# Result rows in four tables by the rank of a token's experts, two of them added early, and the experts' first layer issued one step further ahead

## The reference

```python
x = layernorm(x + attention(x))   # 16 heads of 64, causal, one null key and value, x @ Wo at the end
x = layernorm(x + moe(x))

def moe(xf):                      # xf: 4096 tokens of 128
    scores = softmax(xf @ wg.T)   # 32 experts in 8 groups of 4; the best 4 groups stay,
    w, idx = top 4 of what stays  # and w is divided by its sum
    # every expert takes its first 640 tokens (capacity), in order of the tokens
    h = silu(xe[e] @ w1[e]) * (xe[e] @ w3[e])       # xe: [32, 640, 128]
    y[token] += (h @ w2[e]) * weight of the token
    return y + (silu(xf @ sw1) * (xf @ sw3)) @ sw2  # the shared expert
```

## Time and profile before

| stretch of the trace, us | length | what runs |
| --- | --- | --- |
| 0 to 655 | 655 | attention, router, first scatters |
| 655 to 702 | 47 | last batch's end, first expert |
| 702 to 926 | 224 | 29 experts, 5 scatters each |
| 926 to 960.4 | 34.4 | the tail |

### The profile page before, as it was taken

How to read it: one execution, slowest core, us unless ns; L and a number is a source line. 1 busy time by engine, 2 the same in 40 slices (tenths; PEclk the granted TensorE clock), 3 DMA queues, 4 the chain that set the end, 5 groups by cost and what they waited for, 6 DMA issues and landing times.

```text
span 960.4 us, 26130 instructions
## 1 busy us (share of the span) xinstructions
PE 817.0 (85%) x9489; PEld 594.5 (62%) x9489; DVE 673.9 (70%) x2532; ACT 650.1 (68%) x1262; POOL 681.7 (71%) x580
## 2 busy tenths in 40 slices
PE   4889999999999999999999999873377778786765
PEld 2367777777777777777777777762145555554532
DVE  6667788987987987987897897766255445545417
ACT  3678888888888798898798787864155444444405
POOL 7556565699699689689779869654656576676646
PEclk9799999999999999999999999997789898989979
DMA  5697797743453355345434433133358676566448
GB/s 159 152 297 220 241 249 202 188 121 97 97 147 98 71 140 131 73 108 133 104 90 125 116 80 98 35 91 93 74 117 175 150 168 139 144 152 140 103 157 302
DMA packets 164432, 133.88 MB, mean 139 GB/s; under 512 B 69907, under 2 KB 131654, under 8 KB 163408
## 3 DMA queue, kind: packets, MB, share of 16 engines
q1 hardware_dynamic: 155408, 116.60, 47.4%
q0 software_dynamic: 8896, 15.61, 5.7%
HBM read 31.19 MB, written 39.49 MB: 74 GB/s over the span
## 4 chain that ended last, share of the span: by engine, by line
PE 63%; issue 9%; DVE 7%; DMA 6%; ACT 6%; SPq 5%; another core or an unknown queue 3%; POOL 1%; ACTq 0%; DVEq 0%; POOLq 0%
PE PS L1328 8%; PE PS L1385 6%; PE PS L1359 4%; PE PS L1409 4%; PE PS L1392 4%; PE PS L1390 4%; PE PS L1342 3%; PE PS L1224 3%; PE PS L1411 3%; PE PS L1410 3%; PE PS L1438 3%; PE PS L1439 3%; PE PS L1183 3%; SPq L2503 2%
## 5 line engine op out<-in xcount | busy, mean ns | idle before, releaser
L2328 POOL TENSOR_TENSOR PL<-PF,PH 128x1280 f16<-128x1280 f32 x121 | 317.7, 2626 | 105.6 <-ACT PH L1674 66.6
L1943 DVE CUSTOM_DVE_ANT_0 JUNK<-PS,M 128x256 f16<-128x256 f32 (+3 forms) x512 | 225.3, 485 | 43.6 <-PE PS L1359 40.8
L1668 ACT ACTIVATE PF<-PS 128x512 f32<-128x512 f32 (+1 forms) x384 | 193.2, 520 | 77.3 <-PE PS L1392 74.3
L2371 POOL DMA_INDIRECT y_rows<-BIG,PLACE x150 | 153.0, 1020 | 85.7 <-ACT BIG L1568 48.0
L1674 ACT ACTIVATE PH<-PF 128x1280 f16<-128x1280 f32 x128 | 162.2, 1267 | 0.6
L2361 POOL DMA_INDIRECT xe_rows<-PAY,DEST x128 | 130.2, 1017 | 43.8 <-issue 27.7
L1385 PE MATMUL PS<-Q,K 128*128 128x512 f16 (+3 forms) x512 | 147.9, 299 | 6.9 <-DMA Q<-MROW 3.7
L1409 PE MATMUL PS<-VH,PH 128*128 128x65 f16 x1280 | 140.2, 195 | 11.4 <-DVE Y L1985 7.4
L1411 PE MATMUL PS<-VH,PL 128*128 128x65 f16 x1280 | 140.1, 193 | 0.1
L1410 PE MATMUL PS<-VL,PH 128*128 128x64 f16 x1280 | 140.1, 194 | 0.0
L1409 PEld LDWEIGHTS PS<-VH,PH 128*128 128x128 f16 x1280 | 119.1, 97 | 31.2 <-issue 20.1
(11 more groups left out here) (287 smaller groups left out, 2146.6 us busy)
## 6 DMA issues: line engine op xcount, KB each, us to landing
K<-KH SPq DMA_DIRECT2D x128, 128.0 KB, 2.3
Q<-QH SPq DMA_DIRECT2D x128, 128.0 KB, 2.4
xe_rows<-PAY SPq DMA_DIRECT2D x20, 520.0 KB, 4.1
Q<-xe_rows SPq DMA_DIRECT2D x30, 325.0 KB
K<-KL SPq DMA_DIRECT2D x64, 128.0 KB, 2.3
Q<-QL SPq DMA_DIRECT2D x64, 128.0 KB, 2.4
y_rows<-PAY SPq DMA_DIRECT2D x16, 512.0 KB, 4.9
K<-in_L_ffn_w_dram SPq DMA_DIRECT2D x78, 64.0 KB
```

The costliest lines, as they stand in the source:

```text
L1668: e.activation(PF[:, n % PBUF, c0:c0 + width], PS[:, k, 0:width], ACT.Exp).then_inc(s["c_exp"], 1)
L1943: e.tensor_tensor_reduce(JUNK[:, n_ttr % 2, 0:width], PS[:, base + ab, c0:c0 + width], M0[:, 512 - width:512], 1.0, -3e38, ALU.add, ALU.ma ...
L2328: e.tensor_tensor(PL[:, n % PBUF, :], PF[:, n % PBUF, :], PH[:, n % PBUF, :], ALU.subtract).then_inc(s["c_lp"], 1)
L2371: e.indirect_dma_start(out=y4[:, :], out_offset=bass.IndirectOffsetOnAxis(ap=PLACE[:, x_ % 8, k:k + 1], axis=0), in_=rows_of(x_)[:, k, :], ...
```

## The change

1. **Order of the experts and the row numbers.** `expert(x)` is now 29 - x. The result row is (number of the token's chosen experts whose index is higher) times 4096, plus the token. So `y_rows` is four tables of 4096 rows: table 0 holds each token's result of its highest expert, table 3 that of its lowest. Since the loop goes from high to low, and the experts above 29 take row numbers too without writing them, table 0 is complete after x = 26, table 1 after x = 27. DVE computes the numbers with three new instructions for a batch or half batch ("ahead", "ahead sum", "payi"); POOL's iotas of the payload are gone (four for each batch), one of the setup (TOK) is new.
2. **The tail.** Tables 0 and 1 are loaded by 16 DMAs of 256 KB when they are complete, and DVE adds them to X1 (`share add`, 128x512, both inputs in SBUF). After the last scatter 8 DMAs of 512 KB load tables 2 and 3, half of the bytes of before. PE adds X1 and these two in PSUM; POOL's and DVE's adds are gone, and DVE and ACT read the sum from PSUM.
3. **The loop.** `hidden(x+2)` stands behind `product(x)`, where `hidden(x+1)` stood; `hidden(1)` stands ahead of `product(0)`. Rows split and ring split are of x+3, and the rows of x+4 are loaded ahead of the transpose of x+3. Load ring is still of x+4, so ring split of x+3 now stands one iteration behind its load, where it stood two.

The diff, cut to its core (left out: names, marks, buffers and semaphores, the removed iotas, and ACT's last line, which reads the sum from PSUM):

```diff
@@ -64,7 +64,7 @@
 
 def expert(x_):
 
-    return NE - NA + x_ if x_ < NA else x_ - NA
+    return NE - 1 - x_
@@ -514,6 +514,7 @@
         part("pick", 1)
         yield
         dv("pick sum")
+        dv("ahead sum")
         yield
@@ -522,6 +523,7 @@
                 scatter()
         dv("dest")
         dv("payw")
+        dv("payi")
         yield
@@ -843,22 +846,25 @@
     hidden(0)
     step("set split", 1)
     rows_in(2)
+    hidden(1)
     product(0)
-    hidden(1)
     step("set split", 2)
+    rows_in(3)
     x1_in(1)
-    splits = SPLITS[4:]
+    hidden(2)
+    step("set split", 3)
+    splits = SPLITS[5:]
     forms = list(range(len(WEIGHTS)))
     for x_ in range(1, NE):
-        rows_in(x_ + 2)
-        if NA <= x_ + 2 < NE:
-            step("ring split", x_ + 2)
+        for y_ in range(NA, NA + 2) if x_ == 1 else (x_ + 4,) if x_ + 4 < NE else ():
+            step("load rows", y_)
+        rows_in(x_ + 3)
         if NA <= x_ + 3 < NE:
-            step("load rows", x_ + 3)
+            step("ring split", x_ + 3)
         piece_up()
         product(x_)
-        if x_ + 1 < NE:
-            hidden(x_ + 1)
+        if x_ + 2 < NE:
+            hidden(x_ + 2)
         if NA + 4 <= x_ + 4 < NE:
             step("load ring", x_ + 4)
         if x_ + 1 < NB:
@@ -869,6 +875,12 @@
         for j in splits[0:1]:
             step("set split", j)
         splits = splits[1:]
+        if x_ == NE - 2:
+            for b in range(NB - 1):
+                step("share add", 0, b)
+    step("share add", 0, NB - 1)
+    for b in range(NB):
+        step("share add", 1, b)
@@ -1130,33 +1146,43 @@
...
+    EARLIER = (words_of(flat_of(PF), 2560) + words_of(flat32(PH, 1536), 1536)
+               + words_of(PAY[:, :, :, :].rearrange("p a b r -> p (a b r)"), 2048) + words_of(words(XHL[:, :, :]), 1024)
+               + words_of(VL[:, :, :, :, :].rearrange("p a b c d -> p (a b c d)").bitcast(F32), 1024))
+    FINAL = [t[:, o:o + 1024] for t in (ph2, ph4) for o in range(0, 4096, 1024)]
+    y4_s = y4.rearrange("(k b p f) c -> k b p (f c)", k=TOPK, b=NB, p=128)
@@ -1527,22 +1553,27 @@
 
         def begin(i):
             b, q0, q1 = parts[i]
-            w.wait_ge(s_oc, 5 * NE)
-            w.wait_ge(s_hs, NE)
-            w.wait_ge(s_dacc, len(DENSE))
-            w.wait_ge(s_acc, 2 * (i - 8) + 1)
-            e.matmul(PS[:, i % 8, 0:128 * (q1 - q0)], IDF[:, :],
+            if b == 0:
+                w.wait_ge(s_hs, NE)
+            elif b == 3:
+                w.wait_ge(s_dh, len(DENSE))
+                w.wait_ge(s_dacc, len(DENSE))
+            elif b == 6:
+                w.wait_ge(s_oc, 5 * NE)
+            w.wait_ge(s_share, NB + b + 1)
+            w.wait_ge(s_x2, i - NB + 1)
+            e.matmul(PS[:, BANK[i], 128 * q0:128 * q1], IDF[:, :],
                      X1[:, 4 * b + q0:4 * b + q1, :].rearrange("p q c -> p (q c)"), start=True, stop=False)
 
-        for i in range(8):
+        for i in range(NB):
             begin(i)
         for i, (b, q0, q1) in enumerate(parts):
-            part = PS[:, i % 8, 0:128 * (q1 - q0)].rearrange("p (q c) -> p q c", c=128)
-            w.wait_ge(l_y4[i], 16)
-            e.matmul(part, IDF[:, :], y_of(b)[:, q0:q1, 0, :], start=False, stop=False)
-            e.matmul(part, IDF[:, :], y_of(b)[:, q0:q1, 1, :], start=False, stop=True).then_inc(s_xy, 1)
-            if i == 3:
-                begin(8)
+            if i >= NB:
+                begin(i)
+            w.wait_ge(*landed(TOPK - 1, b))
+            t = slice(128 * q0, 128 * q1)
+            e.matmul(PS[:, BANK[i], t], IDF[:, :], share_of(2, b)[:, t], start=False, stop=False)
+            e.matmul(PS[:, BANK[i], t], IDF[:, :], share_of(3, b)[:, t], start=False, stop=True).then_inc(s_xy, 1)
@@ -2176,6 +2205,31 @@
...
+            elif name == "ahead":
+                b, *half = a
+                q0, q1 = span(*half)
+                w.wait_ge(*(at("index float", b, *half)))
+                wide4 = (128, q1 - q0, 4, 4)
...
+                e.tensor_tensor(AH[:, q0:q1, :, :], chosen(b)[:, q0:q1, :].unsqueeze(3).broadcast_to(wide4),
+                                chosen(b)[:, q0:q1, :].unsqueeze(2).broadcast_to(wide4), ALU.is_lt).then_inc(s["c_dv"], 1)
+            elif name == "ahead sum":
+                b, *half = a
+                q = slice(*span(*half))
+                w.wait_ge(*at("ahead", *a))
+                e.tensor_reduce(AHS[:, q, :].rearrange("p q k -> p (q k)"),
+                                AH[:, q, :, :].rearrange("p q k e -> p (q k) e"), AX, ALU.add).then_inc(s["c_dv"], 1)
+            elif name == "payi":
+                b, *half = a
+                q0, q1 = span(*half)
+                w.wait_ge(*at("ahead sum", *a))
+                for h in half or (0, 1):
+                    w.wait_ge(*at("scat", b - 1, h))
+                w.wait_ge(*at("filled", 0))
+                w.wait_ge(s_const, 1)
+                e.scalar_tensor_tensor(out=PAY[:, q0:q1, :, 128].bitcast(I32), in0=AHS[:, q0:q1, :], scalar=float(N),
+                                       in1=TOK[:, 4 * b + q0:4 * b + q1].unsqueeze(2).broadcast_to((128, q1 - q0, 4)),
+                                       op0=ALU.mult, op1=ALU.add).then_inc(s["c_dv"], 1)
@@ -2220,6 +2274,13 @@
                 dense_times(*a)
             elif name == "dense add":
                 dense_add(*a)
+            elif name == "share add":
+                k, b = a
+                w.wait_ge(*landed(k, b))
+                w.wait_ge(s_dacc, before_in_batch(len(DENSE), b))
+                w.wait_ge(s_share, NB * (k - 1) + b + 1)
+                x1b = X1[:, 4 * b:4 * b + 4, :].rearrange("p q c -> p (q c)")
+                e.tensor_tensor(x1b, x1b, share_of(k, b), ALU.add).then_inc(s_share, 1)
@@ -2227,16 +2288,12 @@
...
-                w.wait_ge(s_pair, i + 1)
                 w.wait_ge(s_x2, i - 2)
-                e.tensor_tensor(sums_of(i, 0)[:, 0:n, :], PS[:, i % 8, 0:128 * n].rearrange("p (q c) -> p q c", c=128),
-                                PR[:, i % 3, 0:n, :], ALU.add).then_inc(s_acc, 1)
-                w.wait_ge(s_acc, 2 * i + 1)
                 w.wait_ge(s_nb, i - 2)
                 for q in range(n):
-                    r = e.bn_stats(st[:, q, :], sums_of(i, 0)[:, q, :])
+                    r = e.bn_stats(st[:, q, :], sum_of(i)[:, q, :])
                 r.then_inc(s_acc, 1)
-                w.wait_ge(s_acc, 2 * i + 2)
+                w.wait_ge(s_acc, i + 1)
@@ -2372,15 +2423,8 @@
                     out=y4[:, :], out_offset=bass.IndirectOffsetOnAxis(ap=PLACE[:, x_ % 8, k:k + 1], axis=0),
                     in_=rows_of(x_)[:, k, :], in_offset=None, bounds_check=last_y4,
                     oob_is_err=False).then_inc(s_ys[x_ % 4], 16)
-        for i, (b, q0, q1) in enumerate(parts):
-            w.wait_ge(l_y4[i], 16)
-            w.wait_ge(s_acc, 2 * (i - 3) + 1)
-            w.wait_ge(s_hs, NE)
-            e.tensor_tensor(PR[:, i % 3, 0:q1 - q0, :], y_of(b)[:, q0:q1, 2, :], y_of(b)[:, q0:q1, 3, :],
-                            ALU.add).then_inc(s_pair, 1)
-            if i:
-                weigh(i - 1)
-        weigh(len(parts) - 1)
+        for i in range(len(parts)):
+            weigh(i)
@@ -2541,13 +2585,22 @@
                 load_ring(*a)
             elif name == "load rows":
                 load_rows(*a)
-        for i, (b, q0, q1) in enumerate(parts):
-            for k in range(4):
-                w.wait_ge(s_ys[k], 80 * len(range(k, NE, 4)))
-            w.wait_ge(s_oc, 5 * NE)
-            w.wait_ge(s_dacc, len(DENSE))
-            f = slice(512 * q0, 512 * q1)
-            e.dma_start(BUF[b][:, f], y4_b[b][:, f]).then_inc(l_y4[i], 16)
+        for b in range(NB):
+            w.wait_ge(l_xa[b], 16)
+        for k in (0, 1):
+            for j in range(4):
+                w.wait_ge(s_ys[j], 80 * len(range(j, NE - TOPK + 1 + k, 4)))
+            for b in range(NB):
+                e.dma_start(share_of(k, b), y4_s[k, b]).then_inc(landed(k, b)[0], 16)
+        w.wait_ge(s_rh, NE)
+        w.wait_ge(s_rl, NE)
+        w.wait_ge(s_gp, NE)
+        w.wait_ge(s_dacc, len(DENSE))
+        for j in range(4):
+            w.wait_ge(s_ys[j], 80 * len(range(j, NE, 4)))
+        for b in range(NB):
+            w.wait_ge(*landed(1, b))
+            e.dma_start(FINAL[b].rearrange("p (k f) -> p k f", k=2), y4_s[2:4, b].rearrange("k p f -> p k f")).then_inc(l_y4[b], 16)
```

67 lines of the change are left out of this document (34 added, 33 removed).

## The result

In 20 runs each, side by side on one chip, the kernel before has a median of 966.47 us and the changed one 957.80 us: a ratio of 0.9945, with an interval of 0.9922 to 0.9969. That is a small gain, under the 2%: 8.7 us, where the terms of the forecast add up to 34.

The account below looks back on a forecast made before the run. It took POOL, waiting for ACT's outs behind a chain through PE's product, to bound the loop, with no engine full. 962.1 - 4 - 24 - 9 + 3 = 928.1, plus 5 for the median: 933 us, range 912 to 960.

Parts of the forecast that it names:

- the loop's -24: 29-expert loop: hidden(x+2) behind product(x) takes silu and times out of the chain, saving 24 us, ends 0 and -32.4.
- the unexplained delay: In the loop, on every second expert, ACT starts outs after 4.12 us of idle although the product's row has ended.
- The floor of 6.50 us for PE: Loop: what remains of PE per expert once the product's waits go, (224.0 - 35.5) / 29, just under POOL's 6.61.
- The chain: Loop before the change: product, outs, silu, times, product wait in a circle; the product idles 35.5 us, 1.22 per expert.
- the row load's move: Loop, SP queue: row loads go one transpose ahead, 1.06 us of issue, cost 0 if the product doesn't wait for rows.
- Rival A: Loop: late start of outs sets the pace, so only start and tail gain; 957 us, chance 0.26.
- Start of the loop: POOL's 8.01 us wait before the scatters of x = 1 shrinks as hidden(1) precedes product(0): -4 us, bounds 0 and -8.
- The share adds: DVE's 16 two-input adds and 4 MB of loads beside POOL's last scatters cost +3 us, bounds 0 and +8.
- The tail: After the last scatter: half the bytes in the first load, PE sets the pace; -9 us, bounds -10 and -4.
- Router on DVE: Routing before the loop: 27 more short DVE instructions, offset by POOL's iotas leaving the path; sum 0, bounds -1 and +1.
- Rival B: Loop: ring split waits for its load, making the kernel slower; 996 us at a landing of 11 us, chance 0.07.
- Rival C: Loop: POOL never waits, the chain was all, -32.4 us there; 919 us in all, chance 0.10.

Follow-up runs that it names:

- the probes: Changed kernel with PE's four matmul groups rerun behind its tail beside scatters and other companions; five rounds beside scatters took 38.1 us on chip 9, 24.8 beside transposes.
- the kernel where only the order was left to hold it: Kernel before, old order, with one of each expert's five scatters: 902.43 us, 0.9788 of before, on chip 12.
- The one pair of runs: One scatter per expert instead of five: in the changed kernel 882.78 us (0.9182, chip 9), in the kernel before 902.43 us (0.9788, chip 12).

## Why the prediction was wrong, and where it was right

- **The step that failed is the loop's -24.** "The loop" gave two ends, 0 if the unexplained delay keeps the pace and -32.4 if POOL never waits, and took three quarters, "since the waits of 2.2 us are those that the chain explains". They weren't. The product's idle time fell from 35.5 to 10.4 us as that paragraph said, and POOL's wait went from 32.4 to 30.4: the loop moved by +0.2 us, or by -2.9 without the 3.1 of the share adds. What held POOL were PE's late signals; they are late because of POOL's own scatters, on the chips where that happens: the same kernel's loop takes 192.8 us on chip 12, with no late signal. It is a loop that closes on itself: ten scatters 0.30 us apart, then a wait of some 2 us in which PE's completions come through, then the outs that they release, then ten scatters. A chain that is removed from PE leaves this as it is. That the hold ends within some 3 us of the last scatter of a run is shown by the probes; that this circle sets the pace of 224 us is argued from them, from the kernel with one scatter and from chip 12. The floor of 6.50 us for PE, on which the three quarters leaned, was not one either: it counted PE's other waits as work, and with one scatter the new order takes 5.25.
- **The chain was read wrongly too.** I closed it as product, outs, silu, times. In the kernel where only the order was left to hold it, the product waits 0.9 us in all, and the circle is rows split, transpose, row load, landing, 6.95 us. The prediction put the row load's move at nothing, as moved issue work, and did not see that it opened this circle. The rows for it were there: ACT waited 1.30 us on a row load in the earlier trace rows. The one pair of runs does not say how the 1.45 us an expert divides between this move and hidden's.
- **Rival A had the number and half of the mechanism**: 957 against a median of 957.80. Late outs set the pace, as it says, but not on all experts, and it had no reason for their lateness. That the number fits to 1 us is in part luck: it took 10 us off the profiled run, where 7.9 came off, and added 5 for the median, where the median lies 3.6 above the new profiled run. The forecast gave it 0.26 and said itself what would show it at the root: a loop over 215 us. It took 224.2.
- **Start of the loop**: -2.4 for -4, within the bounds. That it comes from the step is not shown: with the old order and the four tables the wait was 0.30 us.
- **The share adds**: the last ten scatters went from 9.7 to 12.8 us of busy time, +3.1 for +3. The hit is 0.5 us, 1.46 or 1.50 for 0.97 us, as at 909.84, while DVE's adds run. The trace agrees with the rule of the Trainium skill (GPSIMD Engine Reference, section 8, Key points) on DVE instructions with two SBUF inputs; halving the adds took away 2.5 of the 3.1. Not each of the 16 adds cost a hit.
- **The tail**: -6.2 for -9, within -10 and -4. Loads, landing and the end chain were met to 0.2 us. The 0.4 us for a cold start were too few: it cost 1.8 us, and 1.1 us from PE's last sum to DVE's last statistics were not in the sum.
- **Router on DVE**: 0 for 0, the first scatter moved by 0.2 us. **Rival B** did not come, since the loop is not longer, but its sign did: ACT waits 15.1 us for the ring's loads, 33.4 on chip 12, where the prediction had cost 0. **Rival C's** condition, POOL never waiting, is met on chip 12, where the time before is 47 us lower as well; so even there the gain is 9 us.

## What to carry to other kernels

Before a delay is left unexplained on a path, compare the end of the producer's row with the start of its consumer on several engines: if all consumers of one producer are late together, the producer's signals are late, and shortening the producer's work brings nothing. Bound the gain of a new order by the kernel with the suspect taken out (here four of five scatters), not by the idle time that one chain seems to explain. And when a load moves past a waiting instruction on its queue, ask whether it closed a circle there, before its move is called free.

## What the runs showed of the hardware

- POOL's indirect scatters issued 0.30 us after each other hold back PE's completions on chips 9 and 15 (the probes; on chip 11 the late signals of the loops look the same): signals up to 14.4 us late beside matmuls that need nothing from the scatters, then gaps of up to 2.3 us in PE's issue, and 37.6 to 40.9 us for what takes 24.8. The case's own traces of before and after look like those of these chips. On chip 12 not one recorded signal is late in the loops of seven runs, and the kernel before takes 920 us instead of 965 to 971.
- It is the instruction, not its rows, bytes or writes (six sets of 20 scatters, once on such a chip). With 0.22 us more between two PE's issue was not held over 20 scatters, but signals were at least up to 2.7 us late; with 1.9 us more none was.
- Open: what resource the two share, why it takes some seven scatters to begin, and what sets chip 12 apart. Whether a pause after every few scatters, instead of after each, frees the loop on the other chips was not tried.
